# Graph network kernel: the chunks with one-hot products are spread in another pattern, and the attribute product runs in 64 by 64 tiles

## What is computed

```
e = edge_attr @ enc_edge_w + enc_edge_b
for layer in range(4):
    msg = relu(z[src] + e) + 1e-7
    m = msg * t[layer]
    ex = exp(m - segment_max(m, dst)[dst])
    agg = segment_sum(msg * ex, dst) / segment_sum(ex, dst)
    h = h + relu(layernorm((z + agg) @ w1 + b1)) @ w2 + b2
    z = relu(layernorm(h))
out = layernorm(x + z)
```

## Time and profile before

| what | value |
|---|---|
| median of 3 runs | 3443.28 us (3441.72 to 3448.09) |
| the profiled execution | 3450.53 us, span 3448.7 us |
| busy: PE, DVE, POOL, ACT | 80%, 83%, 68%, 52% of the span |
| mean granted TensorE clock | 0.875 |
| layer 0, first chunk on DVE to chunk 49 | 54.3 to 900.6 us |
| layers 1, 2, 3, first gather to last chunk on DVE | 748.6, 748.7, 737.5 us |

### The profile page before, as it was taken

How to read it: one execution, slowest core, us unless ns; L and a number is a source line. 1 busy time by engine, 2 the same in 40 slices (tenths; PEclk the granted TensorE clock), 3 DMA queues, 4 the chain that set the end, 5 groups by cost and what they waited for, 6 DMA issues and landing times.

```text
span 3448.7 us, 51735 instructions
## 1 busy us (share of the span) xinstructions
PE 2758.4 (80%) x20152; PEld 1420.6 (41%) x20152; DVE 2874.7 (83%) x2835; ACT 1782.7 (52%) x2240; POOL 2358.5 (68%) x2429
## 2 busy tenths in 40 slices
PE   3767676777279999999758999999938999999964
PEld 2333333333144445444434444444415444444433
DVE  5899999999857888888876888888875888888895
ACT  2677775666424444555433444544443545444544
POOL 5777777777357777777627777777735777777752
PEclk7888888889679999999959999999967999999985
DMA  5999999999838999999847999999963999999971
GB/s 146 278 277 297 299 277 266 274 282 297 234 120 265 277 300 299 302 283 294 209 119 212 298 298 292 282 296 294 286 150 125 292 289 294 305 299 296 278 181 40
DMA packets 1050710, 879.63 MB, mean 255 GB/s; under 512 B 912475, under 2 KB 939616, under 8 KB 1018657
## 3 DMA queue, kind: packets, MB, share of 16 engines
q1 hardware_dynamic: 942832, 478.76, 53.8%
q10 hardware_dynamic: 28960, 305.28, 23.6%
q0 software_dynamic: 78672, 92.29, 11.0%
HBM read 557.36 MB, written 318.70 MB: 254 GB/s over the span
## 4 chain that ended last, share of the span: by engine, by line
DVE 29%; PE 27%; SPq 12%; POOL 11%; issue 8%; ACT 6%; DMA 6%; POOLq 0%; ACTq 0%; DVEq 0%
PE X L552 21%; POOL gath L492 10%; SPq L362 9%; DVE decay L925 6%; DVE state_all L956 5%; DMA keep<-keep_dram 5%; DVE rows_all L911 4%; PE X L533 3%; DVE one_hot L1020 3%; DVE X L930 3%; DVE state_all L940 2%; SPq L352 2%; SPq L341 1%; ACT X L671 1%; ACT msg L669 1%
## 5 line engine op out<-in xcount | busy, mean ns | idle before, releaser
L492 POOL DMA_INDIRECT gath<-z_table,idx x2296 | 2238.3, 975 | 857.3 <-issue 710.0
L552 PE MATMUL X<-one_hot,z_parts 128*64 128x512 fp8e5 x10650 | 1228.7, 392 | 111.7 <-DVE one_hot L1020 94.4
L552 PEld LDWEIGHTS X<-one_hot,z_parts 128*64 128x64 bf16 x10650 | 607.0, 113 | 759.6 <-DVE one_hot L1020 128.1
L552 PE MATMUL X<-between,z_parts 128*64 128x512 fp8e5 x6750 | 749.1, 381 | 0.0
L681 ACT ACTIVATE decay<-X 128x1024 f32<-128x1024 f32 (+2 forms) x216 | 209.1, 968 | 916.1 <-DVE X L930 893.5
L533 PE MATMUL X<-attr,enc_edge 128*128 128x512 f32 x824 | 478.6, 709 | 243.1 <-DVE state_all L956 235.8
L552 PEld LDWEIGHTS X<-between,z_parts 128*64 128x64 bf16 x6750 | 376.0, 110 | 377.5 <-issue 51.1
L911 DVE STREAM_TRANSPOSE rows_all<-state_all 128x1024 f32<-128x1024 f32 (+3 forms) x432 | 505.8, 1171 | 17.3 <-DMA rows_table<-rows_all 9.8
L940 DVE TENSOR_TENSOR_SCAN state_all<-decay,state_all,X 128x1024 f32<-128x1024 f32 (+2 forms) x216 | 468.2, 2167 | 20.0 <-ACT X L686 20.0
L925 DVE TENSOR_TENSOR_SCAN decay<-X,decay 128x1023 f32<-128x1023 f32 (+2 forms) x216 | 477.1, 2209 | 7.9 <-DVE decay L923 0.2
L956 DVE TENSOR_TENSOR_SCAN state_all<-decay,state_all,X 128x1024 f32<-128x1024 f32 (+2 forms) x216 | 467.9, 2166 | 0.0
(11 more groups left out here) (160 smaller groups left out, 1689.9 us busy)
## 6 DMA issues: line engine op xcount, KB each, us to landing
rows_table<-rows_all SPq DMA_DIRECT2D x784, 256.0 KB
attr<-attr_t SPq DMA_DIRECT2D x196, 512.0 KB
one_hot<-one_hot_dram ACTq DMA_DIRECT2D x48, 1920.0 KB
between<-one_hot_dram ACTq DMA_DIRECT2D x45, 1920.0 KB
one_hot<-one_hot_dram ACTq DMA_DIRECT2D x48, 1280.0 KB, 8.6
one_hot_dram<-one_hot SPq DMA_DIRECT2D x31, 1920.0 KB, 10.4
between<-one_hot_dram ACTq DMA_DIRECT2D x45, 1280.0 KB
one_hot_dram<-one_hot SPq DMA_DIRECT2D x31, 1280.0 KB
```

The lines of the kernel that those rows point to most:

```text
L492: pool.indirect_dma_start(out=gath[s][:, n * F:(n + 1) * F], out_offset=None, in_=z_table, in_offset=bass.IndirectOffsetOnAxis(ap=idx[:, c ...
L552: last = nc.tensor.matmul(x[h * F:(h + 1) * F, BANK:CH], z_parts[:, i * GB + k, third, :], bank[:, i, k, h * BANK:(h + 1) * BANK], start=F ...
```

## The change

It does two things.

1. `FIRST_CHOSEN` becomes the chunks of 4 to 47 whose number is 1, 3, 4, 6 or 7 modulo 8, 28 in all, and `CHOSEN` is 0, 1 and the same, 30 in all. So layer 0 uses 28 banks where it used 23; layers 1 to 3 use 30 where they used 31; 30 banks are built where 31 were. Of eight chunks in the walk five are chosen, as before in layers 1 to 3 (before, 0, 2, 4, 5 and 6 modulo 8; in layer 0 four, the even ones).
2. `edge_product` no longer multiplies by a block-diagonal 128x128 weight. The attributes of the first 512 columns of both halves lie on partitions 0 to 63, one half behind the other, and those of the second 512 columns on 64 to 127. A full chunk takes four f32 matmuls with 64 rows, 64 columns of weight and 512 columns of data, one for each bank and half; a short chunk takes two. The bytes loaded per chunk are the same; the host lays them out in the new order.

```diff
-FIRST_CHOSEN = [c for c in range(NCH) if c % 2 == 0 and 4 <= c <= 48]
-CHOSEN = [c for c in range(NCH) if c < 2 or (c % 2 == 0 or c % 8 == 5) and 4 <= c <= 48]
+FIRST_CHOSEN = [c for c in range(4, 48) if c % 8 in (1, 3, 4, 6, 7)]
+CHOSEN = [0, 1] + FIRST_CHOSEN
...
-                blk, at = block_of(c)
-                sp.dma_start(attr[g % SLOTS][:, 0:width(c)], attr_t[blk * P:(blk + 1) * P, at:at + width(c)])\
+                row, at, parts = attr_place(c)
+                n = HALVES * min(width(c), BANK)
+                sp.dma_start(attr[g % SLOTS][0:parts, 0:n], attr_t[row:row + parts, at:at + n])\
...
-                for b in range(0, width(c), BANK):
-                    last = nc.tensor.matmul(X[g % XS][:, b:b + BANK], enc_edge2[:, :], attr[s][:, b:b + BANK],
-                                            start=True, stop=False)
+                w = min(width(c), BANK)
+                for b in range(-(-width(c) // BANK)):
+                    for h in range(HALVES):
+                        last = nc.tensor.matmul(X[g % XS][h * F:(h + 1) * F, b * BANK:b * BANK + w], enc_edge2[b * F:(b + 1) * F, :],
+                                                attr[s][b * F:(b + 1) * F, h * w:(h + 1) * w], start=True, stop=False)
                 last.then_inc(attr_used, 1)
```

More of the change, by code:

```diff
@@ L112, in block_of, with attr_place @@
     return STARTS[c] // CH, STARTS[c] % CH
+def attr_place(c):
+    blk, at = block_of(c)
+    if width(c) == CH:
+        return blk * P, 0, P
+    return blk * P + at * HALVES // CH * F, at * HALVES % CH, F
 def keep_chunks(b):
@@ L156, in gnn_kernel @@
         eps_col = sb("eps_col", [P, 1])
-        enc_edge2 = sb("enc_edge2", [P, P])
+        enc_edge2 = sb("enc_edge2", [P, F])
         edge_bias = sb("edge_bias", [P, 1])
@@ L332, in _ @@
             for h in range(HALVES):
-                sp.dma_start(enc_edge2[h * F:(h + 1) * F, h * F:(h + 1) * F], enc_edge_w).then_inc(consts_landed, 16)
+                sp.dma_start(enc_edge2[h * F:(h + 1) * F, :], enc_edge_w).then_inc(consts_landed, 16)
             sp.dma_start(edge_bias[:, :], enc_edge_b).then_inc(consts_landed, 16)
@@ L1206 @@
     src_b = np.stack([streams(src, 0)[:, c * CH + BANK:(c + 1) * CH] for c in BANKS]).reshape(P, SUB)
-    attr_s = chunked(streams(attr, 0)).transpose(1, 0, 3, 2).reshape(NBLK * P, CH)
+    attr_h = streams(attr, 0)
+    attr_s = np.zeros((NBLK * P, CH), attr.dtype)
+    for c in range(NCH):
+        row, at, parts = attr_place(c)
+        w = min(width(c), BANK)
+        for b in range(parts // F):
+            for h in range(HALVES):
+                attr_s[row + b * F:row + (b + 1) * F, at + h * w:at + (h + 1) * w] = \
+                    attr_h[h, STARTS[c] + b * BANK:STARTS[c] + b * BANK + w].T
     nxt = list(range(1, LAYERS)) + [0]
```

## The result

| kernel | median, us | lowest to highest | ratio, 95% interval |
|---|---|---|---|
| before | 3443.28 | 3439.86 to 3448.09 | |
| changed | 3456.05 | 3452.32 to 3461.39 | 1.0041, 1.0028 to 1.0053 |

The changed kernel is 0.4% slower. The forecast was 3386 us, with a range that ended at 3422. The changed kernel's profiled execution took 3459.49 us, with a span of 3457.7, 9 us longer than before. In it all lines have moved by 10: L933 is the first DVE instruction of a chunk, L543 the attribute product, L562 the one-hot products, L669 ACT's `penalties`, L360 the load of `keep`.

What follows compares the result with a forecast made beforehand. POOL's gathers were taken to bound layers 1 to 3, DVE layer 0 behind chunk 27. -14.6 - 22.8 - 14 - 6 = -57.4 us, from 3450.5 to 3393.1, scaled to a median of 3386 us; range 3357 to 3422.

Steps and rivals of the forecast that it cites:

- What bounds the kernel: Whole kernel: POOL at 1.25 us a gather bounds layers 1 to 3; DVE bounds layer 0 behind chunk 27.
- Layer 0: Walk of layer 0: 40 gathers fewer on POOL, DVE then sets the time; -14.6 us together.
- the rival feared ahead of L1030: Layer 0 waits for PE: 11 neighbouring chosen pairs each cost 3 us; 3419 us, chance 0.07.
- First gather to chunk 8: Start of the walk, layers 1 to 3: 139.5 us for 148.97, 146.17 and 146.10, together -22.8 us.
- Chunks 8 to 48: Middle of the walk, layers 1 to 3: 553 us for 557.28, 560.00 and 555.72, together -14 us.
- the long turns of PE: At chunks 3-4 and 6-7 modulo 8: one PE turn of 19.4 us, making DVE late by up to 4.8 us twice.
- Keep waits at every even chunk: Rival for layers 1 to 3: 113 us for eight chunks, middle piece +22 where forecast -14; 3422 us, chance 0.06.
- the first piece: First gather to chunk 8 in layers 1 to 3, forecast at -22.8 us together.
- the tail: Chunks 48 to 53 in layers 1 to 3, forecast at -6 us together.
- Chunks 48 to 53: End of the walk, layers 1 to 3: next layer's first bank load starts a chunk earlier; -3, -3 and 0 us.
- The attribute product: PE's f32 product in 64 by 64 tiles: 2.4 us a chunk for 1.91, hidden by POOL, no time change.
- the serial rival: Tiles run one after the other on PE, 3.8 us a chunk; 3528 us, as median 3521, chance 0.09.

## Why the prediction was wrong

- **What bounds the kernel.** POOL at 1.25 us a gather as the floor under layers 1 to 3 was right, and shown: 551 us in two kernels with different patterns. But before the change it did not bind yet: POOL has 11% of the chain that ended last, and 32% once `keep` is early in the same kernel. Taking `keep`'s wait away alone brought chunks 8 to 48 from 557 to 551 us, and the prediction had that row ahead of it: the earlier trace rows has the 4.78 us.
- **Layer 0**: -14.6 us forecast, -12.9 measured at chunk 49 (900.63 and 887.69). The idle time that the rival feared ahead of L1030 did not come. The sum is right, its pieces only in part: -4.2 us at the start of chunk 4 as forecast, -2.4 for -6.2 from chunk 4 to 26, -6.4 for -4.2 behind it. So the closeness is in part luck.
- **First gather to chunk 8**: 139.5 us forecast; 145.7, 145.3 and 145.4 measured, for -22.8 us only -4.9. With `keep` early it is 139.9, 142.1 and 140.8, near the working; but the old pattern with `keep` early has 143.3, 143.0 and 143.1, so most of that gain is `keep`'s and not the change's.
- **Chunks 8 to 48**: this is the step that failed. The prediction took 553 us, "nearer the floor since the loads of the banks no longer come in threes", and let the long turns of PE cover part of "the keep waits that this doesn't cover". It measured 567.44, 569.44 and 562.61: +26.5 us where -14 stood.
- **What the runs show in its place.** Banks in threes were not the harm. A bank that ACT puts out whole just ahead of a `keep` load in SP's queue is. Two go out whole in eight chunks in either pattern, and what changed is the order. In the old pattern one goes out at the messages of chunks 5 modulo 8, where a `keep` load stands close by. In the kernel before, at chunk 21 of layer 1, SP's issue and then ACT's:

```profile
1331.65 2.63 SPq L352 DMA_DIRECT2D keep<-keep_dram  x2
```

```profile
1333.91 0.33 ACTq L724 DMA_DIRECT2D one_hot<-one_hot_dram  x1
1334.33 0.40 ACTq L724 DMA_DIRECT2D between<-one_hot_dram  x1
```

  The load went first in 10 of 12 such cases, by 0.7 to 2.5 us, was issued in 1.8 to 3.4 us, and DVE waited 0 to 4.3 us at the next chunk. In the other two, with the bank first, it waited 5.9 and 6.2 us, PE's waits at chunk 5 notwithstanding. In the new pattern, at 3 modulo 8, the bank goes first in 12 of 15 cases; in 11 of these the load, or the stores ahead of it, take 9.4 to 13.3 us to issue, and in all 12 DVE waits 5.4 to 8.7 us at the next chunk. In the three where the load still goes first (chunk 11 of each layer) DVE waits 5.7, 2.2 and 0.2 us. The other whole bank, at 4 before and at 6 now, goes out 8 to 13 us behind the nearest `keep` load. With this order, and with PE's waits gone, DVE's mean wait at 5 modulo 8 went from 6.8, 5.1 and 6.1 us to 0, that at 4 from 2.5, 2.3 and 2.7 to 7.0, 6.1 and 5.7, and that at 2 from 2.1, 2.4 and 2.0 to 3.6 in each layer.
- **The rival that held** was "*Keep waits at every even chunk* now that PE's are gone, 113 us for eight chunks". Its pace is what was measured, 567.44 / 5 = 113.5, 113.9 and 112.5 us, though not its reason: the wait is not only uncovered but larger, 355.2 us for 231.6. It got 0.06, and its sum, 3422, kept the gains of the other two pieces, which the same wait takes: another 17.9 us of the first piece and 4.8 of the tail. With these it comes to 3445, no change.
- **Chunks 48 to 53**: -6 us forecast, -1.2 measured (41.7, 42.0 and 35.65). With `keep` early 39.5, 38.2 and 35.7.
- **The attribute product**: costed at nothing, with 2.4 us a chunk in bounds from 1.0 to 3.8. It takes 1.02 us (1297.96 to the next start at 1298.98), the lower bound: the four tiles run beside each other. It does not stand on the path, as forecast, and the serial rival is out. The rows show no idle time where the tiling mode changes: the transposes start 1.02 us behind the attribute product, the next product 0.59 us behind them, and the one-hot products 1.02 us behind that. By the rule on draining in the Trainium skill, TensorEngine Tiling (Array Packing), Tiling Modes, there should be a drain at each of these; one that is short enough to lie inside these intervals isn't ruled out.
- **The sum with the cause taken away.** -57.4 us was forecast from the profiled execution. The changed kernel with `keep` early has a span of 3392.1 us where the kernel before has 3448.7: -56.6. That is not the change's worth: the old pattern with `keep` early is at 3417.4, so 31.3 of the 56.6 us are the earlier load's and 25.3 the change's. The sum had counted most of the end of `keep`'s waits as a gain of the change: -14 us in chunks 8 to 48, where both patterns take 551 to 553 us once `keep` is early.

What stays open: what the tiles give alone at 3440 us, how much a third `keep` buffer is worth there, and why the same chip runs TensorE at two paces.

## What to carry to other kernels

Where two waits alternate, price the removal of one by what the other costs when nothing covers it any more, and follow in which order the queues issue afterwards: here the large loads moved by a chunk, came ahead of the small one instead of behind it, and DVE's longest waits came to stand behind it. A small load in an ordered queue behind stores is late by what other queues put on the DMA engines at that moment, so it is issued a step earlier before the pattern of the large loads is changed. And where the floor is one engine's instruction count, spreading the work of another moves nothing in that stretch: with `keep` out of the way both patterns take 551 us there.

## What the hardware showed unexpectedly

- The issue of two `keep` loads of 128 KB on SP's queue took 1.8 to 5.5 us with no bank just put out by ACT's queue, and 9.7 to 11.8 us (five of six) just behind a whole bank of 3200 KB.
- A DMA share of 0.97 or 0.99 did not mean a bound: the changed kernel moved the same bytes in 567 us at 0.97 and in 551 us at 1.00, the kernel before in 557 us at 0.99 and in 551 us at 1.00.
- The next instruction started 1.02 us behind the start of eight records of f32 products in 64 by 64 tiles, and 1.91 us behind four records over the full array.
- One program had two paces on TensorE: the kernel before took about 3440 us, or 4582 to 4716 us. The mean granted clock was 0.875 in its profile at 3450 us and 0.782 to 0.802 in the profiles of the long runs, which are of other kernels. Two chips showed both.
